# Re-timing the hand-written step tables of a fused convolution kernel: projections at chunk ends, earlier matmul turns, an earlier chain for the generated weights, and a ninth tap without gathers in the whole last image

## The reference

```python
x = x + L0(gn(x))   # gn: group norm, 32 groups of two channels
x = x + L1(gn(x))

# L0: 1x1 conv 64->128; a small network on the image's mean makes 3x3 depthwise weights
xh = w_in @ x + b_in
kernels = relu(mean(xh) @ kg_w1.T + kg_b1) @ kg_w2.T + kg_b2
y = depthwise3x3(xh, kernels)
out0 = w_out @ (y * tanh(softplus(y))) + b_out

# L1: deformable 3x3 conv: 9 taps per pixel, each at its own bilinear position and with a mask
offset = conv3x3(x, w_off); mask = sigmoid(conv3x3(x, w_mask))
val[k] = bilinear(x, position(k) + offset[k]) * mask[k]      # k = 0..8
z = w_1x1 @ concat(sum_k w_def[k] @ val[k], offset, mask)
out1 = silu(batchnorm(z))
```

## Time and profile before

| | before |
|---|---|
| median of three runs | 5542.11 us (5542.05 to 5542.53) |
| the profiled execution | 5550.28 us, its span 5548.3 us |
| POOL busy | 4053.5 us, 73% of the span |
| DVE busy | 4494.7 us, 81% |
| PE busy | 4469.9 us, 81%, mean granted clock 0.81 |
| ACT busy | 2602.9 us, 47% |
| gathers issued by POOL | 4236 |

### The profile page before, as it was taken

One profiled execution on the slowest core, in us unless ns is written; L12 is line 12 of the kernel. 1 busy time (PEld: TensorE's weight loads), 2 busy tenths in 40 slices (PEclk: granted clock), 3 DMA queues, 4 the chain that ended last, 5 costly groups with the idle time before them and its releaser, 6 DMA issues.

```text
span 5548.3 us, 46071 instructions
## 1 busy us (share of the span) xinstructions
PE 4469.9 (81%) x14762; PEld 2004.9 (36%) x14762; DVE 4494.7 (81%) x5306; ACT 2602.9 (47%) x3591; POOL 4053.5 (73%) x4243
## 2 busy tenths in 40 slices
...
GB/s 117 92 118 134 106 132 122 120 132 106 143 106 132 123 112 140 105 131 122 115 137 104 133 123 120 131 105 140 112 130 123 108 143 104 131 116 115 122 108 100
DMA packets 279695, 667.35 MB, mean 120 GB/s; under 512 B 76447, under 2 KB 116762, under 8 KB 277210
## 3 DMA queue, kind: packets, MB, share of 16 engines
...
...
## 4 chain that ended last, share of the span: by engine, by line
PE 38%; DVE 27%; POOL 18%; issue 11%; ACT 4%; DMA 2%; DVEq 0%; ACTq 0%; SPq 0%; POOLq 0%
POOL gat L507 18%; PE yo_ps L776 12%; PE tap_ps L776 7%; DVE gat L1370 6%; PE z_ps L698 6%; DVE pairs L1349 5%; DVE conv_ps L1240 5%; DVE hat_s L1397 4%; PE tap_ps L692 3%; PE conv_ps L571 2%; DMA gat<-patch_table,ixu 2%; PE conv_ps L646 2%; PE conv_ps L590 1%; DVE uc L1247 1%; PE xh_ps L758 1%
## 5 line engine op out<-in xcount | busy, mean ns | idle before, releaser
L507 POOL DMA_INDIRECT gat<-patch_table,ixu x4236 | 4045.2, 955 | 1480.6 <-issue 1264.6
L1370 DVE TENSOR_TENSOR gat<-gat,wgt_ps 128x1024 f32<-128x1024 f32 x1059 | 1283.4, 1215 | 445.1 <-DMA gat<-patch_table,ixu 438.1
L1349 DVE TENSOR_REDUCE pairs<-gat 128x256 f32<-128x1024 f32 x1024 | 1239.5, 1210 | 0.0
L776 PE MATMUL yo_ps<-hat_s,hat_image 128*128 128x512 f32 x1860 | 1009.1, 697 | 7.4 <-issue 7.4
L776 PE MATMUL tap_ps<-hat_s,hat_image 128*128 128x512 f32 x1860 | 887.2, 626 | 0.0
L692 PE MATMUL tap_ps<-ident,pairs 128*128 128x128 f32 x2048 | 393.5, 324 | 569.7 <-DVE pairs L1349 569.7
L1040 ACT ACTIVATE val<-tap_ps 128x512 f32<-128x512 f32 x512 | 303.2, 592 | 1094.8 <-PE tap_ps L692 1094.7
L776 PEld LDWEIGHTS yo_ps<-hat_s,hat_image 128*128 128x128 f32 x1860 | 418.5, 233 | 604.5 <-issue 594.5
L1240 DVE SCALAR_TENSOR_TENSOR conv_ps<-xh,kb,conv_ps 128x1024 f32<-128x1024 f32 x480 | 617.4, 1286 | 12.7
L692 PEld LDWEIGHTS tap_ps<-ident,pairs 128*128 128x128 f32 x2048 | 271.8, 163 | 884.0 <-DVE pairs L1349 709.0
L776 PEld LDWEIGHTS tap_ps<-hat_s,hat_image 128*128 128x128 f32 x1860 | 357.4, 201 | 422.2 <-issue 410.1
...
## 6 DMA issues: line engine op xcount, KB each, us to landing
gat<-patch_table,ixu POOLq DMA_INDIRECT x4236, 2.7
...
hat_image<-patch_table SPq DMA_DIRECT2D x144, 128.0 KB
out<-n_z SPq DMA_DIRECT2D x128, 128.0 KB, 2.4
...
```

The lines of the kernel that those rows point to most:

```text
L507: pool.indirect_dma_start(gat[:, k, t * 2 * REC:(t + 1) * 2 * REC], None, table_rows, bass.IndirectOffsetOnAxis(ixu[:, i, k, t:t + 1], 0)) ...
L776: m = pe.matmul(hat_sums[t % 2][:, :], hat_image[:, q // NCH % 2, i, t, :], hat_s[:, i, :], start=(i == 0), stop=(i == HI - 1))
L1349: dve.tensor_reduce(total, gat[:, k, :].rearrange("p (t x c h) -> p t c x h", t=TILES, x=2, h=2), mybir.AxisListType.XY, ALU.add).then_inc ...
L1370: dve.tensor_tensor(patch, patch, wk.rearrange("p (n h) -> p n h", h=2).unsqueeze(2).to_broadcast([128, TILES * 2, C, 2]), ALU.mult).then_ ...
```

## The change

The tables are rewritten; the work stays the same but for three things: the last image computes its ninth tap on PE in chunks 5 and 6 too (8 gathers fewer), ACT instead of DVE makes the normalised input of image 1's `hidden`, and ACT loads the table set with silu explicitly ahead of tanh and of the first offsets.

- `project` moves from the first tap of the next chunk to the end of its own (`KK` is 9, the end), and `residual` from unit 3 to unit 2.
- The four turns move from units 1, 3, 5, 7 to 1, 2, 4, 6; their `hat_post` from 4, 6, 8, 9 to 3, 5, 7, 9; `hat_y` from 1 to 0.
- `x_stats` moves wholly into chunk 5, the chain from `x_mean` to `kernels` from chunk 7 to chunk 6, and `hidden` starts at the end of chunk 6 instead of in the middle of chunk 7. The chain's small results move to the bank `tap_ps[1]`.
- At the start, the offsets, pixels and points of image 0's chunk 1 come ahead of image 1's generated weights and its `hidden`.

```diff
-PLAN_BLOCK0 = ((1, "project"), (3, "residual"), (3, "convolve 0"), (4, "convolve 1"), (5, "convolve 2"), (6, "exp"),
-               (7, "ln"), (8, "tanh"), (8, "finish"))
+PLAN_BLOCK0 = ((2, "residual"), (3, "convolve 0"), (4, "convolve 1"), (5, "convolve 2"), (6, "exp"), (7, "ln"), (8, "tanh"), (8, "finish"), (KK, "project"))
...
 def has_hat(q):
 
-    return q < B * NCH and q % NCH in (HATS if q >= NCH else HATS0)
+    return q < B * NCH and (q >= (B - 1) * NCH or q % NCH in (HATS if q >= NCH else HATS0))
...
-            return (tap_ps[0], tap_ps[1])[n] if isinstance(n, int) and n < 2 else tr_ps
+            return tap_ps[0] if is_first(n) else tap_ps[1]
...
                 if n > 1:
-                    pe.wait_ge(rec_done, n * NCH + 1)
+                    pe.wait_ge(hat_scaled, HT * hats_before((n - 1) * NCH - 2))
...
+                if t == 1 and q % NCH == NCH - 1 and q // NCH + 2 < B:
+                    pe.wait_ge(kernel_dve, (q // NCH + 2) * KERNEL_STEPS + 8)
...
+            offsets(0, 1, 1)
             x_mean(1)
             x_var(1)
+            first_pixels(0, 1)
             x_norm(1)
...
-                steps = {"project": lambda b, g, i: project(b + 1, g - 1),
+                steps = {"project": lambda b, g, i: project(b + 1, g),
...
-                if n > 1:
+                if n > 0:
                     if s == 0:
                         act.wait_ge(kernel_dve, n * KERNEL_STEPS + 7)
...
                 if n > 0:
+                    act.preload_act_table_set("silu_and_others")
                     act.wait_ge(ln_done, n * NCH + s * 2 + 2)
...
             x_norm(1)
+            first_points(1)
             kernels(1)
-            for s in range(NCH // 2):
-                hidden(1, s)
-            first_points(1)
             dve.sem_inc(math, 2 * MATH_STEPS)
```

More of the change, by code:

```diff
@@ L58 @@
 PLAN_START = (
[L59 to L62, removed]
@@ L63 @@
[L63 to L64 removed]
+    ((2, "first_offsets 2"), (4, "first_offsets 3"), (5, "first_pixels 1"), (6, "first_offsets 4"), (6, "first_points 2"), (8, "first_offsets 5"),
+     (KK, "first_pixels 2")),
+    ((3, "first_offsets 6"), (4, "first_offsets 7"), (5, "first_pixels 3"), (6, "first_points 3")),
+    ((6, "first_points 4"),),
 )
[L66 removed]
+PLAN_NORM = ((2, "residual"), (4, "group_mean"), (5, "group_var"), (6, "normalise"), (8, "finish"))
@@ L67 @@
 PLAN_PREPARE = (
[L68 to L71, removed]
@@ L72 @@
-    ((1, "x_mean"), (1, "points 3"), (2, "x_var"), (2, "points 4"), (2, "next_indices"), (3, "x_norm"), (3, "points 5"),
-     (4, "hidden_units"), (5, "kernel_taps"), (6, "kernels"), (6, "hidden 0"), (7, "hidden 1"), (8, "hidden 2"), (8, "finish"), (KK, "hidden 3")),
-)
-PLAN_HAT = ((1, "hat_rows"), (1, "hat_up 0"), (3, "hat_up 1"), (4, "hat_post 0"), (5, "hat_out 0"), (5, "hat_up 2"), (6, "hat_post 1"),
-            (7, "hat_out 1"), (7, "hat_up 3"), (8, "hat_post 2"), (KK, "hat_post 3"))
-PLAN_NEXT_HAT = ((1, "hat_y"), (3, "hat_part"), (4, "hat_x"), (6, "hat_mask"), (8, "hat_weigh"), (KK, "hat_select"))
+    ((1, "last_row"), (1, "offsets 0"), (2, "to_table 0"), (2, "x_stats 0"), (3, "to_table 1"), (4, "offsets 1"), (4, "to_pixels 0"), (4, "x_stats 1"),
+     (5, "to_table 2"), (6, "x_stats 2"), (6, "to_table 3"), (7, "to_pixels 1"), (8, "to_table 4"), (8, "finish"), (KK, "x_stats 3")),
```

34 lines of the change are left out of this document (21 added, 13 removed).

## The result

The changed kernel takes 5715.9 us (median of four, 5707.8 to 5718.1) against 5542.3 before: ratio 1.031, 95% interval 1.0297 to 1.0322. It is slower by 174 us, where 57 us less was forecast, and 156 us above the range's end. The profiled execution took 5707.83 us, its span is 5705.7.

What follows compares the result with a forecast made beforehand. POOL bounds the kernel: 117 us + gathers x 1.26 + waits for transposes. Images 1 to 14 give -35 us, last image -10, start -12: -57; with 8.2 from profiled run to median, 5550.3 becomes 5485 us, range 5430 to 5560.

Steps and rivals of the forecast that it cites:

- the sum: POOL's lateness at chunk 5 per image: 17 + 176 + 11 = 204 us against 201.6 of gathers, 2.4 late.
- the lead: From POOL's first gather of chunk 0 to DVE's start of it: 20.2 us before, 17 forecast (11 to 22).
- chunk 7: Falls from 53.2 to 45.5 us as its 7.28 wait for turn 3 goes, giving the lead 7.7 back.
- the length of turn 3: Turn 3 on PE in chunks 1 to 3: taken as 4.56 us, 6.29 at a granted clock of 0.50.
- the release: From DVE's start of chunk 4 until transposes let POOL go on: 11.9 us before, about 11 forecast.
- chunks 0 to 3: DVE's time for the four: 176 us (173 to 181), 41 for chunk 0, 45 each after; 174.4 before.
- The bound: Whole kernel: time is 117 us + gathers x 1.26 + POOL's waits for transposes; POOL is idle for nothing else.
- Start and end: Start: -12 us (-5 to -21.4), DVE's chunk 0 begun near 119. Last image: 8 gathers fewer, -10 us.
- The wait at `project`: Ends of chunks 1 to 3: DVE waits 2.7 us for tanh, replacing 3.4 for turn 3 at `hat_post 3`.
- Chunk 6: Grows from 48.9 to 53 us with new waits of about 6 each at `x_norm` and `kernels`, 12 together.
- the waits at the chunk ends outgrow the one removed: Rival: turn at 6.29 makes chunks 1 to 3 46.7, lead 22, sum 214 us; 5621 us, chance 0.21.
- The rule of the Trainium skill: ACT's table switches in tanh's chain: 2.66 us each, chain some 2.8 longer, sum 11 more; table-switch rival 5633 us, chance 0.01.

Runs made afterwards that it cites:

- start_last: Kernel before with only the new order of the start and the last image's ninth tap without gathers: 5509.8 us, ratio 0.9946.
- project_early: Changed kernel with the norm chain and `hidden` back at their old taps and ln and tanh at unit 6: 5453.9 us, ratio 0.9834.
- short_turn: Changed kernel with turn 3 of chunks 0 to 3 cut to three of its five matmuls (ninth tap incomplete there): 5590.5 us, ratio 1.0078.
- early_tanh: Changed kernel with ln and tanh at unit 6, right behind exp, `project` left at the chunk's end: 5519.8 us, ratio 0.9961.
- warm: Changed kernel with three more matmuls on PE ahead of `hat_x`'s in chunks 0 to 3, no result changed: 5730.6 us, ratio 1.0324.
- chain_sl: start_last with `x_stats`, the norm chain and `hidden` at their new taps, turns and `project` as before: 5564.1 us, ratio 1.0042.

## Why the prediction was wrong

Three steps of the sum failed: the lead (chunk 7), the length of turn 3, and a place of waiting that it did not have. By the means over images 2 to 13 (the release too is 11.9 in the mean) the three terms are 24.9 + 180.8 + 11.9 = 217.6 against 200.8: POOL is 16.8 us late where 2.4 was forecast. Of the 14.4 between them the lead has 7.9 (24.9 for 17) and chunks 0 to 3 have 4.8 (180.8 for 176). The rest of the 19.7 that were measured is mostly a wait ahead of the lead, for which the sum had no term.

**The bound was right.** POOL's account held to the us, and spans less POOL's net waits agree: 5443 before (with the 10 for the 8 gathers taken off), 5423 changed, 5426 in start_last, 5425 in project_early; the 17 to 20 us between the first and these are the shorter mean gather. This mean goes from 950 to 956 ns from run to run (955.0 before, 955.8 in short_turn), some 20 us over all gathers, and no run shows why; a difference of that size between two kernels needs its waits beside it. Hence every loss had to show as a wait of POOL, and did.

**Start and end were right.** DVE begins chunk 0 at 116.8 (119 forecast). The start gave 21.4 - 5.6 = 15.8 net against 12, the end its 10.

**Chunks 0 to 3: the mechanism was right, one term was too small.** The wait at `project` took the place of that at `hat_post 3`, as forecast. The chain's pieces in chunk 1 of image 7, on PE, where the second pair's transposes waited for DVE:

```profile
2655.86 1.11 PE L689 MATMUL tap_ps<-ident,pairs 128*128 128x128 f32 x4 [3.34 <-DVE pairs L1351]
...
2661.35 6.89 PE L775 MATMUL tap_ps<-hat_s,hat_image 128*128 128x512 f32 x10
...
2668.16 1.12 PE L755 MATMUL xh_ps<-cat,hat_sel 43*128 43x512 f32 x2
```

and on ACT:

```profile
2669.91 0.60 ACT L1042 ACTIVATE val<-tap_ps 128x512 f32<-128x512 f32 x1 [6.54 <-PE tap_ps L689]
2670.53 1.28 ACT L931 ACT_TABLE_LOAD   x1
2671.82 1.15 ACT L931 ACTIVATE uc<-uc,one_c 128x1024 f32<-128x1024 f32 x1
...
2674.28 1.06 ACT L942 ACTIVATE uc<-uc 128x1024 f32<-128x1024 f32 x1
```

`hat_post 1` ends 26.65 into the chunk (26.6 forecast); the copy to tanh's end takes 5.43 (5.49). But turn 3 begins 1.1 us after `hat_post 1`'s end (0.6), and takes 6.89 where the sum had 4.56: tanh ends at 41.8, and not 39.0. DVE was at `project` at 37.6 (36.3), as it had first waited 1.2 for `hat_mask`. Mean over chunks 1 to 3: turn 3 6.34, wait 4.2, chunk 46.3 (45 forecast), with 41.8 for chunk 0: 180.8 for the four, at the end of the range I gave (173 to 181). The failed step is the choice within it: turn 3's 4.56 was taken from its old place, where PE came from work, and the rows held the other duration too, 6.29 for a turn behind transposes that had been waited for in the kernel before:

```profile
2584.54 1.11 PE L692 MATMUL tap_ps<-ident,pairs 128*128 128x128 f32 x4 [5.70 <-DVE pairs L1349]
```

The new place is of that kind. The prediction also took 6.29 for a turn at 0.50, and so for the most that it could be. Its stretch ends before that turn does; over the whole turn the granted clock was 0.72:

```profile
2588.54:2594.83 6.29, 6.29 (x13) 2.53 (x11) 6.29 (x7) 3.43 (x3) 4.77 (x6) 0.72 0.38 107
```

PE's clock in the stretches up to and past turn 3, in the changed kernel:

```profile
2646.90:2651.40 4.50, 4.49 (x11) 1.82 (x11) 4.46 (x5) 0.00 (x0) 3.56 (x4) 1.00 0.35 106
2651.40:2656.00 4.60, 1.26 (x4) 0.43 (x4) 4.57 (x5) 1.41 (x2) 3.38 (x5) 0.98 0.31 96
2656.00:2661.30 5.30, 4.93 (x20) 1.92 (x20) 5.23 (x6) 2.08 (x3) 4.08 (x5) 0.50 0.38 111
2661.30:2668.20 6.90, 6.90 (x13) 2.80 (x11) 6.90 (x8) 2.06 (x2) 5.06 (x6) 0.65 0.35 105
2668.20:2672.90 4.70, 3.89 (x23) 1.77 (x22) 1.82 (x2) 2.96 (x3) 1.88 (x2) 1.00 0.32 88
```

Turn 2 ran at 1.00 (2.4 GHz); PE then worked 1.26 us of 4.6, the clock fell to 0.50 (1.2 GHz), and turn 3 ran mostly at that level. That each us of the turn is a us of the chunk is shown by short_turn, and that the place of tanh is the larger part of the loss by early_tanh: in chunk 0 turn 3 takes 4.56, and DVE still waits 3.8 at `project`. Why the clock was low ahead of turn 3 is not shown: warm filled the idle time and it fell all the same.

**Chunk 6 was about right, chunk 7 was the wrong step.** Chunk 6 takes 50.9 (53). DVE's waits in chunk 6 of image 7:

```profile
DVE mr L1192 <- ACT std L877: 7.9, 1, 7.9
...
DVE kb L1201 <- PE tap_ps L547: 4.0, 1, 4.0
```

11.9 together, where 12 was taken (about 6 each, so the sum fits better than its parts). In chunk 7 the prediction let the wait of 7.28 go, and named PE's late entry (5 to 6 us), but left it out of the 45.5. DVE's waits in chunk 7 of image 7:

```profile
DVE hat_wy L1406 <- PE yo_ps L775: 14.4, 2, 9.6
DVE xh_ps L1390 <- PE xh_ps L755: 5.7, 1, 5.7
```

Before, DVE's waits in this chunk were 17.2 us in all, the 7.28 among them; these went, and 22.1 came, 20.1 of them in the two lines. The reason on PE:

```profile
2896.86 3.78 PE L568 MATMUL conv_ps<-n_z,w_in 64*128 64x512 f32 x4 [2.17 <-ACT n_z L899]
2900.43 1.91 PE L741 MATMUL xh_ps<-cat,hat_sel 43*128 43x512 f32 x2
2902.28 5.90 PE L775 MATMUL yo_ps<-hat_s,hat_image 128*128 128x512 f32 x10
```

`hidden 1` waits for ACT's `n_z`, which stands behind the copies and silu of the chunk before; `hat_y` and turn 0 stand behind `hidden 1`, and turn 0 begins 14.5 us into the chunk. Chunk 7 is 55.5 in the mean, 10 above the forecast, and the lead 24.9 in place of 17, above the 22 that was to be the worst. The 7.7 us that chunk 7 was to give back fail even with the turns and `project` at their old places: it takes 53.7 in chain_sl, where the chain and `hidden` alone are moved, and 53.6 in start_last, where they are not.

**One place of waiting was missed.** The sum counted lateness at chunk 5 alone. POOL also waits in chunk 0's gathers, for the late transposes of chunk 7: 3.9 net an image, more than half of it at the first gather and so ahead of the lead.

**The rivals.** The one that came is "the waits at the chunk ends outgrow the one removed": with both of its mishaps its sum was 214, and 217.6 was measured (219.3 in image 7). It had been given 0.21, and 5621 us; the wait at chunk 0 is not in it. The rule of the Trainium skill, "ScalarE: Activation LUTs", section "What ACT_TABLE_LOAD costs", would have ended on the right side for a wrong reason: that page's load of 1283 ns is here as 1.28, but the next instruction starts 1.29 after the load's start (2670.53 to 2671.82), so its drain of 1380 ns does not show here. The interaction itself was in the prediction's chain (tanh behind the copy of the third pair, this copy behind turn 3). What the prediction did not work out is what the two moves are worth apart: the early turns alone gain 43 us, `project` alone costs nothing, and the two together lose 128 against start_last.
